# A two-layer transformer sandwich on one core: the opening put in a new order, with the work of head 0 on VectorE

## What is computed

```python
    residual = h
    x = (h - mu) * jax.lax.rsqrt(var + EPS) * ln_g + ln_b
    q = (x @ wq.T + bq).reshape(b, s, N_HEADS, D_K)
    k = (x @ wk.T + bk).reshape(b, s, N_HEADS, D_K)
    v = (x @ wv.T + bv).reshape(b, s, N_HEADS, D_K)
    q = rope(q)
    k = rope(k)
    attn = jnp.einsum('bihd,bjhd->bhij', q, k) * scale
    attn = softmax(where(causal, -inf, attn))
    o = jnp.einsum('bhij,bjhd->bihd', attn, v).reshape(b, s, N_HEADS * D_K)
    return o @ wo.T + bo + residual
```

## Time and profile before

| | |
|---|---|
| median of 3 runs | 585.52 us (584.88 to 586.61) |
| the profiled execution | 582.6 us |
| its span, first to last instruction | 580.6 us |
| busy: TensorE matmul / weight load | 532.5 us / 362.8 us |
| busy: VectorE / ScalarE / GpSimd | 475.3 / 385.7 / 380.3 us |
| mean granted TensorE clock | 0.99 of full |

### The profile page before, as it was taken

The page is one execution under the profiler, slowest core; times in us unless marked ns, Lnnn a source line. Parts: engine busy times, 40 slices in busy tenths (PEclk is TensorE's granted clock), DMA queues, the critical chain, the costliest instruction groups (busy, mean ns, idle before and its releaser), DMA issues.

```text
span 580.6 us, 11367 instructions
## 1 busy us (share of the span) xinstructions
PE 532.5 (92%) x4178; PEld 362.8 (62%) x4186; DVE 475.3 (82%) x889; ACT 385.7 (66%) x841; POOL 380.3 (65%) x331
## 2 busy tenths in 40 slices
PE   6669999999999999999997889899999999999895
PEld 2336666666666666666665455466688778657573
DVE  7989998999999999898997887677637896767656
ACT  4486879688787787768778756576666466556221
POOL 1777888899999798878879379631324453434432
PEclk9889999999999999999999999999999999999998
DMA  8235554646564344682535524023110000000002
GB/s 295 79 86 109 97 126 92 116 101 134 94 139 87 60 79 69 153 152 51 87 60 113 156 73 146 11 63 87 37 37 1 2 1 1 0 1 2 1 1 73
DMA packets 98455, 44.62 MB, mean 77 GB/s; under 512 B 88288, under 2 KB 90720, under 8 KB 98400
## 3 DMA queue, kind: packets, MB, share of 16 engines
q1 hardware_dynamic: 97408, 43.35, 33.3%
q10 hardware_dynamic: 992, 0.55, 0.3%
HBM read 21.86 MB, written 1.05 MB: 39 GB/s over the span
## 4 chain that ended last, share of the span: by engine, by line
PE 67%; DVE 14%; POOL 7%; ACT 6%; issue 5%; DMA 1%; SPq 0%; POOLq 0%; ACTq 0%; DVEq 0%
PE bank L1552 59%; PE bank L1729 5%; POOL qkl L565 2%; DVE turned L1129 2%; DVE parts L1147 1%; PE bank L1593 1%; DVE vl L1155 1%; POOL rr L561 1%; DVE stats L982 1%; DVE turned L1325 1%; POOL turned L561 1%; ACT bank L724 1%; DVE nmax L1117 1%; DMA x<-in_x 1%; DVE w_all_l L1061 1%
## 5 line engine op out<-in xcount | busy, mean ns | idle before, releaser
L1552 PE MATMUL bank<-xTh,w_all_h 128*128 128x512 f16 (+2 forms) x392 | 130.0, 332 | 5.4 <-DVE xT L1049 2.6
L1552 PE MATMUL bank<-xTl,w_all_h 128*128 128x512 f16 (+2 forms) x392 | 129.8, 331 | 0.0
L1552 PE MATMUL bank<-xTh,w_all_l 128*128 128x512 f16 (+2 forms) x392 | 129.8, 331 | 0.0
L565 POOL TENSOR_TENSOR qkl<-turned,qkh 128x512 f16<-128x512 f32 (+1 forms) x44 | 55.2, 1254 | 98.3 <-ACT qkh L849 98.1
L535 POOL TENSOR_TENSOR rr<-turned 64x512 f32<-64x512 f32 x63 | 88.3, 1402 | 27.5 <-DVE turned L1129 23.5
L545 POOL TENSOR_TENSOR qkl<-rr,qkh 128x512 f16<-128x512 f32 x64 | 76.6, 1202 | 22.9 <-ACT qkh L746 20.0
L724 ACT ACTIVATE bank<-bank,nmax 128x128 f32<-128x128 f32 (+3 forms) x128 | 64.0, 500 | 41.1 <-DVE nmax L1117 40.6
L536 POOL TENSOR_TENSOR rr<-turned 64x512 f32<-64x512 f32 x63 | 82.6, 1311 | 3.7
L849 ACT ACTIVATE qkh<-turned 128x512 f16<-128x512 f32 (+1 forms) x44 | 27.6, 628 | 59.0 <-DVE turned L1325 59.0
L1147 DVE SCALAR_TENSOR_TENSOR parts<-bank,rscaled,parts 128x128 f16<-128x128 f32 (+3 forms) x128 | 64.1, 543 | 0.5 <-ACT parts L735 0.4
L1117 DVE TENSOR_REDUCE nmax<-bank 128x1 f32<-128x128 f32 (+3 forms) x128 | 57.2, 481 | 4.3 <-PE bank L1593 3.5
(11 more groups left out here) (223 smaller groups left out, 1467.1 us busy)
## 6 DMA issues: line engine op xcount, KB each, us to landing
stage<-in_per_head SPq DMA_DIRECT2D x16, 512.0 KB, 4.1
xa<-in_codes SPq DMA_DIRECT2D x32, 128.0 KB, 2.8
stage<-in_packed SPq DMA_DIRECT2D x12, 256.0 KB, 3.1
stage<-in_scales SPq DMA_DIRECT2D x12, 256.0 KB, 3.7
pT<-parts SPq DMA_TRANSPOSE x128, 2.8
stage<-in_w1T SPq DMA_DIRECT2D x2, 512.0 KB, 4.1
x<-in_x SPq DMA_DIRECT2D x4, 128.0 KB, 2.5
rope<-in_ropes ACTq DMA_DIRECT2D x1, 512.0 KB, 8.0
```

Source lines behind the costliest of these rows:

```text
L565: pool.tensor_tensor(il[n % 2][0:rows, :], inter[0:rows, n % 2, :], ih[n % 2][0:rows, :], ALU.subtract).then_inc(g_il, 1)
L1552: last = pe.matmul(dst, l, r, start=start and i == 0, stop=stop and i == 2, skip_group_check=skip)
```

## The change

1. The row tiles of batch 1 are issued by two queues, 0 and 2 by SP, 1 and 3 by ScalarE. SP then loads weight piece 0, the rope table, the three bias vectors, piece 1, the rows of batch 0 and pieces 2 and 3.
2. VectorE makes both halves of the rotation of unit 0 (four instructions) and both `qkl` of unit 0; GpSimd begins with unit 1.
3. The low parts of the weights are made half by half from a table, `LOW_HALVES_AT`; TensorE waits for the half it needs.
4. Mean and spread of batch 0 are sums made by ScalarE (`other_spread0`, eight passes with an accumulator), and GpSimd makes the reciprocal roots with a power (`norm0`), for batch 1's residual too.
5. Batch 0 is normalised at the end of step -1 and turned whole in step 0, through the two `acc_bank`s; VectorE scales its halves in the steps 0 and 1.
6. In step 0 ScalarE makes `qkh` of the next k between the second and the third part of the probabilities.
7. `open_sums` is gone: the first product of each sum opens its bank (`start=True`).

```diff
-X0_NORM_AT = {0: (OTHER, "nrm"), 6: (FIRST, "xa"), 11: (OTHER, "xa")}
+X0_NORM_AT = {6: (FIRST, "xa"), 11: (OTHER, "xa")}
-X0_TURN_AT = {1: 0, 2: 1}
+X0_TURN_AT = {0: 0, 1: 1}
+LOW_HALVES_AT = {-1: ((), ((0, 1), (2, 0))), 0: (((1, 1),), ((3, 0),)), 1: (((2, 1),), ((4, 0),)), 2: (((3, 1),), ((5, 0),)),
+                 3: (((4, 1),), ((5, 1),)), **{s: (((GROUP + i, 0),), ((GROUP + i, 1),)) for i, s in enumerate(LATE_LOWS)}}
...
-            for t in range(TPB):
+            for t in (0, 2):
                 row = FIRST * TPB + t
                 sp.dma_start(x[:, row, :], x_tok[:, row, :]).then_inc(s_first[t], 16)
-            for j in range(4):
-                load_w(j)
+            load_w(0)
+            sp.dma_start(rope[:, :, :], ropes.rearrange("f p s -> p f s")).then_inc(s_rope, 16)
+            for dst, src in ((bias_q, bqT), (bias_k, bkT), (bias_v, bvT)):
+                sp.dma_start(dst[:, :], src).then_inc(s_small, 16)
+            load_w(1)
             load_x(OTHER)
+            load_w(2)
+            load_w(3)
...
+            def norm0(i, b, var, scale, eps):
+
+                n = 2 * NORM0_ORDER.index(i)
+                pool.tensor_scalar(var0[:, i, :], var, scale, eps, ALU.mult, ALU.add).then_inc(g_var0, 1)
+                pool.wait_ge(g_var0, n + 1)
+                pool.tensor_tensor(rstd0[:, i, :], var0[:, i, :], minus_half[:, 0:TPB], ALU.pow).then_inc(g_var0, 1)
+                pool.wait_ge(g_var0, n + 2)
+                pool.tensor_tensor(shift0[:, i, :], less_mean0[:, b, :], rstd0[:, i, :], ALU.mult).then_inc(g_norm0, 1)
...
+            def other_spread0():
+                tiles = range(OTHER * TPB, (OTHER + 1) * TPB)
+                act.wait_ge(s_x[OTHER], 16)
+                for t in tiles:
+                    last = act.activation(xa[:, t, :], x[:, t, :], ACT.Identity, scale=-1.0 / D,
+                                          accum_out=less_mean0[:, OTHER, t % TPB:t % TPB + 1])
+                last.then_inc(a_mean0, 1)
+                act.wait_ge(a_mean0, 1)
+                for t in tiles:
+                    last = act.activation(xa[:, t, :], x[:, t, :], ACT.Square, bias=less_mean0[:, OTHER, t % TPB:t % TPB + 1],
+                                          accum_out=square0[:, t % TPB:t % TPB + 1])
+                last.then_inc(a_square0, 1)
...
                     for q in range(TPB):
+                        if s == 0 and q == 2:
+                            high_qk(s + 1, 1)
                         high_p(s, q)
...
-            low_w(0)
+            half_low_w(0, 0)
...
-            low_w(1)
+            half_low_w(1, 0)
...
-                dve.tensor_tensor(rr[0:HALF, 1, :], cos_a[HALF:P], sin_b[HALF:P], ALU.subtract)
-                dve.tensor_tensor(rr[HALF:P, 1, :], cos_b[HALF:P], sin_a[HALF:P], ALU.add).then_inc(d_rot, 1)
+                for w, part in enumerate((slice(0, HALF), slice(HALF, P))):
+                    dve.tensor_tensor(rr[0:HALF, w, :], cos_a[part], sin_b[part], ALU.subtract)
+                    dve.tensor_tensor(rr[HALF:P, w, :], cos_b[part], sin_a[part], ALU.add).then_inc(d_rot, 1)
+                dve.wait_ge(d_rot, 2)
+                for w in range(2):
+                    dve.wait_ge(a_qkh, w + 1)
+                    dve.tensor_tensor(qkl[:, 0, w, :], rr[:, w, :], qkh[:, 0, w, :], ALU.subtract).then_inc(d_qkl, 1)
...
-                if w == 1 and u - 2 in X0_TURN_AT:
-                    pe.wait_ge(d_xT, KC + X0_TURN_AT[u - 2] + 1)
...
-                    last = product(acc_bank[t // 2][:, t % 2 * D:t % 2 * D + D], os_, ws, False, False, skip=True)
+                    opens = u in (0, GROUP, DONE) and t % 2 == 0
+                    last = product(acc_bank[t // 2][:, t % 2 * D:t % 2 * D + D], os_, ws, opens, False, skip=True)
...
+                if s == 0:
+                    turn_norm0(OTHER)
...
+                if s == -1:
+                    keep_warm(1)
-
-            def open_sums(banks=acc_bank):
-
-                for a in banks:
-                    pe.matmul(a[:, :], identb[:, :], zerob[:, :], start=True, stop=False, skip_group_check=True)
```

More of the change, by code:

```diff
@@ L401, in rotations, with halves_done, lows_done @@
         def rotations(u, w):
-            return 2 * u + w if u else 1
+            return 2 * u + w - 1
+        def halves_done(j, half):
+            return LOW_HALVES.index((j, half)) + 1
+        def lows_done(j):
+            return max(halves_done(j, half) for half in range(2))
         def there(u):
@@ L1766, in gate_up, with opens_sum @@
                     beside(k + w)
+            def opens_sum(n, i, t):
+                of_unit = n - RUN2 if RUN2 <= n < RUN3 else n - RUN4
+                first = of_unit % (RUN2_HALF if n < RUN3 else RUN4_HALF) == 0 if of_unit >= 0 else n in (RUN1, RUN3)
+                return first and i == 0 and t % 2 == 0
             def down(n, weights, rows):
```

190 lines of the change are left out of this document (94 added, 96 removed).

## The result

| | before | changed |
|---|---|---|
| median, first comparison (7 runs each) | 586.61 us (584.88 to 588.44) | 582.62 us (582.01 to 583.53) |
| ratio, 95% interval | | 0.9937 [0.9918, 0.9955] |
| again, later (23 and 12 runs) | 585.80 us | 582.88 us, 0.9956 [0.9937, 0.9974] |
| the profiled execution | 582.6 us | 582.5 us |
| its span | 580.6 us | 580.7 us |

The change makes the kernel faster, by 2.9 us against the median that stood at the beginning and by 2.9 to 4.0 us in two comparisons on one chip each. The forecast was 6.1. One of the 23 runs took 932.56 us at a mean granted clock of 0.557 and is left out of the ratio.

The account below looks back on a forecast made before the run. TensorE, busy 92% of the span, was taken as the bound, with much of its idle time in an opening chained over other engines. Opening 5.2 plus zeroing 0.9 gave 6.1 us: 585.5 to 579.4, range 577.5 to 582.8.

Parts of the forecast that it names:

- Row tiles on two queues: Opening: the last row tile lands at 4.8 us, so xT starts at 8.55 instead of 9.76, gain 1.2.
- One half before the rotation: Before unit 0's rotation: one low half instead of two, products start at 12.4 instead of 14.14, gain 1.7 so far.
- head 0 on VectorE: Unit 0's rotation: four additions at 0.67 us each, scores at 19.0 instead of 23.37, gain 4.4.
- ScalarE's passes: Opening: eight passes over batch 0, 3.6 us, end at 15.4 before rr's first half at 16.2, and cost nothing.
- Rival B: Unit 0's additions: GpSimd's small instructions hold VectorE up, scores 2.0 later, gain 4.1, time 581.4; chance 0.12.
- Steps 0 to 3: After unit 0's scores: VectorE is the late one, unit 4's scores at 59.1 instead of 64.48; gain taken as 5.2.
- rival C: Steps 0 to 3: VectorE bounds for longer, 0.6 more per step, 2.4 of the gain goes, 581.8; chance 0.07.
- GpSimd's power in step 2: Step 2, before unit 3's rotation: about 2 us extra on GpSimd, hidden, as that rotation ends at 46.8 and is used at 48.
- The zeroing: The 14 zeroing matmuls dropped: four lie on the chain, 4 x 0.216 = 0.9 us, bounds 0 and 2.6.
- rival D: Opening: TensorE's clock falls in three waits and stays at 1.2 GHz until unit 2, 8.9 us added, 588.3; chance 0.04.
- The base: Whole kernel: the profiled 582.6 stood 2.9 under the median, so 6.1 off takes the median from 585.5 to 579.4.

Follow-up runs that it names:

- c2: The changed kernel itself, unchanged, timed and profiled again: 582.88 us, ratio 0.9956 to the kernel before.
- d4: The changed kernel, unchanged, profiled once more: scores of unit 4 at 63.72 us; no median is given.
- e4: The changed kernel with all four row tiles on SP's queue and only the two small vectors on ScalarE's: 580.96 us, ratio 0.9942.
- e10: The changed kernel with row tiles on SP's queue, 12 zero products behind unit 0's scores, one early low half, and 8 opening zero products instead of 16: 580.95 us.
- e1: The changed kernel with the small vectors ln_g and ln_b issued ahead of the row tiles on ScalarE's queue: 582.44 us, ratio 0.9949.
- e7: The changed kernel with step -1's two late low halves made before unit 1's rotation products: 582.10 us, ratio 0.9965.
- e2: The kernel before without its 14 zeroing matmuls, each sum opened by its first product: 585.76 us, ratio 1.0002.
- e9: The changed kernel with the other batch's eight statistics instructions put back on VectorE, their result written over unread: 583.78 us, ratio 0.9968.
- e3: The changed kernel with twelve zeroing matmuls put back at their six later places: 583.18 us, ratio 0.9966.

## Why the prediction was right and wrong

The direction was right, and the measured 582.62 lies within the range (577.5 to 582.8), at its edge. (The range's own terms, 582.2 and 577.9 with 0.8 us either way, would give 577.1 to 583.0.) The size was not: the forecast of 579.4 took 6.1 us off, and 2.9 to 4.0 went. Two steps failed, the row tiles and the steps 0 to 3. The way through head 0 was right. By the steps:

- **Row tiles on two queues (xT at 8.55).** Failed: 10.93, 10.67 in c2, 11.30 in d4; a loss of some 2.4 us at every later point. The sentence that failed is "the small vectors, which competed with the fourth tile, are now behind it": they were behind it, and VectorE multiplies them ahead of the rows. I had walked the tiles to 4.8 (right: mean and variance done at 5.30) and never walked `ln_b`, the next thing that VectorE waits for. This is about half of the loss: with the vectors in time (e4) xT still comes at 9.82, since the loop of zeros, which the prediction let end at 7.9, ends at 9.27. In the changed kernel's three profiles it ends at 8.61, 8.87 and 9.13; 7.9 is the earliest end in the five profiles of the kernel before, so this base was lucky too. Only with both mended (e10) is xT at 8.74. The Trainium skill, "DMA: Bandwidth & Descriptors", section "Issuing engines are not separate DMA queues", says that more issuing engines bring only sequencer time; the runs agree in size: with two queues the last tile's statistics start at 4.48 to 4.80 us (changed, c2, d4), with one at 5.40 (e4), and an issue takes 0.4. But with one the vectors are not waited for at all. That the 512 KB of weight piece 0, now issued earlier on SP's queue, are what delays the last of ScalarE's is an inference from e1 and e4; no run moved that piece alone.
- **One half before the rotation; head 0 on VectorE; ScalarE's passes.** Right. From xT to the products of the rotation 3.95 us (3.85 predicted), the four `rr` 0.68 to 0.70 each (0.67), from products to scores 6.85 (6.6). Rival B did not come. ScalarE's eight passes ended at 17.77 (15.4 predicted), before the first half of `rr` was there to be copied (18.77), and cost nothing.
- **Steps 0 to 3.** Mis-sized by 1.5 us: unit 0 to unit 4 takes 41.62 at full clock, 40.1 predicted; the kernel before took 41.1. The steps of units 1 and 2 last 10.64 and 10.73 us in c2, against 10.1 and 10.0. That is rival C at some 60% of its price. The term that was too small is the low half at 0.62: beside GpSimd's additions it took 1.16 to 1.42, and TensorE waits for it three times, 5.0 us. The earlier trace rows showed the wait on xT as 2.6 us, and I counted it as gone; the low halves took its place. The Trainium skill, "SBUF — State Buffer", section "SBUF: two separate sides", with its lock for whole instructions, fits these numbers. I applied it to the four additions, beside which GpSimd had only instructions on 4 columns, and not to the halves, beside which it has its whole rotation. That the halves' length by itself makes the 1.5 us is not shown: in e7 the first pair took 1.20 and unit 1 came no earlier.
- **GpSimd's power in step 2, "hidden".** Partly wrong. Three instructions on 4 columns took 2.6 us there (44.72 to 47.34) instead of about 2, GpSimd's last qkl of unit 3 ended at 55.38, and the scores came at 55.48 behind 1.01 us of idle TensorE, where 0.16 is usual. From the timeline of GpSimd in the changed kernel:

```profile
44.72 0.19 POOL L575 TENSOR_SCALAR var<-square 128x4 f32<-128x4 f32 x1
44.99 1.01 POOL L577 TENSOR_TENSOR rstd<-var,minus_half 128x4 f32<-128x4 f32 x1
46.08 1.26 POOL L579 TENSOR_TENSOR shift<-less_mean,rstd 128x4 f32<-128x4 f32 x1
...
53.11 2.27 POOL L570 TENSOR_TENSOR qkl<-rr,qkh 128x512 f16<-128x512 f32 x2
```

- **The zeroing.** Mis-sized: 0.9 predicted, at most 0.6 by e2.
- **The clock (rival D).** It did not double a step, but it is worth 1.3 to 1.6 us where it falls behind the wait of 2.6 us (unit 0 to unit 4 in 42.92 us instead of 41.62; 30 products in 4.11 us instead of 2.65). In the kernel before it costs more, and more often: two falls and 0.78 in 24 to 36 us in every profile, and in two of five a longer first fall, worth 2.3. So a part of what the change gains is likely that TensorE's waits of 5.1 and 2.9 us are gone; the prediction, which moved only starts and ends, gave nothing for that. How large this part is stays open.
- **The base.** "It stood 2.9 under the median, so the median goes from 585.5": the step subtracts from the median a gain worked out on a profile in which two losses to the clock were missing, the longer first fall and the one at 325 us (1.1 us on the mean at unit 4, 1.2 behind it). It does no harm as long as the change leaves these alone, but profile against profile the gain at unit 4 is -0.2 us, while the means (65.54 of five, 63.82 of three) give 1.7.

Summed at unit 4, the mean of 63.8 against 59.1: 2.4 from xT, 0.3 from the way to unit 0, 1.5 from the steps behind it, 0.5 from the clock in one of three profiles. Between the 1.7 us at unit 4 and the 2.9 to 4.0 of the medians lies, first, that the eight profiled executions themselves differ by more: their times have means of 584.7 (before, five) and 582.6 us (changed, three), 2.1 apart. Then, the five of the kernel before lie about 1 us below most of its medians (585.5 to 585.8). Eight profiles that scatter by more than 1 us don't settle more than that.

## What to carry to other kernels

Walk every input that the first instructions wait for, the 1 KB vectors too, and not only the large one that ended the wait before: a transfer moved to a second queue pushes back what is behind it there. Where a wait goes, look for the next semaphore of the same instruction, and where VectorE and GpSimd work side by side, price both with the durations they have there, not with the shortest row: one of them pays. Before a profile is used as a base, compare its own time with the runs: one that lies below them all may lack a loss that the median has. Compare kernels at the same granted clock too, not only by their medians.

## What the runs showed of the hardware

- A transfer of 1 KB landed 6.25 us after its issue (5.99 to 6.62 in c2, e9 and d4), while the other queue's large loads were under way.
- The zero loop of 16 products of 512 columns took 4.95 to 6.34 us from one profile to the next (4.95 and 6.29 in two of the kernel before, 5.68, 5.94 and 6.20 in three of the changed one) while the records give a granted clock of 1.00 for the stretch. Its first products start 0.43 us apart, as at the lower level, and the later ones 0.22; after how many the pace changes, some 7 to 13, differs from one execution to the next.
- The same program falls to the lower clock or not from one execution to the next: behind the 2.6 us wait at 24 us in four of six profiles of the changed opening with that wait (changed, e1, e3, e4 at 0.86; c2 and d4 at 1.00), and at some 325 us (0.91 or 1.00 in the stretch 320 to 340) in both kernels, for 1.2 us of the time.
- Two low parts of 512 columns on VectorE took 1.20 us without GpSimd beside them (e7) and 2.37 beside its addition (changed). In e9, with the addition begun just as long behind them, they took 1.21 and the addition 2.24 instead of 1.26.
